# 1/rms of the first network handed over the partitions through DRAM, and its hidden products taken in later turns

## What is computed

```python
neighbor_sum = jnp.einsum('bnm,bmd->bnd', adjacency, x)
agg = epsilon * x + neighbor_sum
h = jnp.einsum('bnd,dh->bnh', agg, W1) + b1          # H = 512
h = jax.nn.silu(h * jax.lax.rsqrt(mean(h * h) + eps) * rms_weight)
out = jnp.einsum('bnh,hd->bnd', h, W2) + b2
x = _layernorm(x + out)
```

## Time and profile before

| | |
|---|---|
| runs | 1186.98 us median (1185.79 to 1189.19) |
| profiled execution | 1185.8 us, span of its instructions 1183.8 us |
| TensorE busy | 1129.8 us, 95% of the span |
| VectorE, ScalarE, GpSimd busy | 73%, 62%, 50% |
| mean granted TensorE clock | 0.984 of full speed |
| stage one | from 40.4 us (first `neighbours`) to 433.5 us |
| stage two | 433.5 us to 493 us |
| stage three | 494 us to the end |

### The profile page before, as it was taken

How to read it: one execution, slowest core, us unless ns; L and a number is a source line. 1 busy time by engine, 2 the same in 40 slices (tenths; PEclk the granted TensorE clock), 3 DMA queues, 4 the chain that set the end, 5 groups by cost and what they waited for, 6 DMA issues and landing times. The chain is left out here.

```text
span 1183.8 us, 24192 instructions
## 1 busy us (share of the span) xinstructions
PE 1129.8 (95%) x7851; PEld 1026.6 (87%) x7851; DVE 867.6 (73%) x2564; ACT 736.1 (62%) x1328; POOL 593.3 (50%) x528
## 2 busy tenths in 40 slices
PE   7899999999999879799999999999999999999984
PEld 7799999999999769678889899898989898989874
DVE  3378877777777713126878888888888888888984
ACT  3444455555555432156677778787878777787765
POOL 1044443434343226424565757575666666675754
PEclk9999999999999999979999999999999999999988
DMA  4123322232322134511011212121212121120001
GB/s 154 54 72 98 100 90 90 90 94 95 98 90 64 54 120 163 169 39 55 30 54 37 73 38 73 37 74 38 73 38 64 47 58 53 41 69 29 10 18 45
DMA packets 46962, 82.58 MB, mean 70 GB/s; under 512 B 5172, under 2 KB 15224, under 8 KB 46584
## 3 DMA queue, kind: packets, MB, share of 16 engines
q1 hardware_dynamic: 46840, 81.05, 21.7%
HBM read 55.34 MB, written 25.69 MB: 68 GB/s over the span
## 5 line engine op out<-in xcount | busy, mean ns | idle before, releaser
L162 POOL TENSOR_TENSOR rstd<-ve,minus_half 128x4 f32<-128x4 f32 x128 | 153.5, 1200 | 150.0 <-DVE ve L1012 144.3
L162 POOL TENSOR_TENSOR r_rms<-ms,minus_half 128x4 f32<-128x4 f32 x32 | 32.3, 1010 | 236.5 <-DVE ms L976 236.5
L454 PE MATMUL bank<-w,s 128*128 128x128 f32 x1024 | 135.1, 275 | 0.4 <-DVE y L990 0.4
L454 PEld LDWEIGHTS bank<-w,s 128*128 128x128 f32 x1024 | 126.9, 192 | 3.5 <-issue 0.5
L1322 POOL TENSOR_TENSOR edge_adj<-edge,atc 128x512 f32<-128x512 f32 x32 | 40.8, 1275 | 101.8 <-ACT edge L828 101.8
L755 ACT ACTIVATE s<-hn,cols 128x512 f32<-128x512 f32 x128 | 84.9, 712 | 10.9 <-DVE hn L983 10.3
L983 DVE SCALAR_TENSOR_TENSOR hn<-bank,cols,rv 128x512 f32<-128x512 f32 x128 | 86.8, 737 | 1.0 <-ACT rv L159 0.6
L149 PE MATMUL bank<-agg_hi,w_hi 128*128 128x512 f32 x192 | 86.9, 452 | 0.0
L1002 DVE BATCH_NORM_STATS2 stats<-y 128x6 f32<-128x128 f32 x384 | 82.7, 277 | 2.6 <-POOL y L1354 2.5
L155 PE MATMUL bank<-at,x_rows 128*128 128x128 f32 x512 | 71.3, 284 | 9.6 <-ACT x_rows L902 6.0
L155 PEld LDWEIGHTS bank<-at,x_rows 128*128 128x128 f32 x512 | 67.1, 199 | 14.1 <-ACT x_rows L902 7.3
(11 more groups left out here) (192 smaller groups left out, 3450.4 us busy)
## 6 DMA issues: line engine op xcount, KB each, us to landing
at<-in_at SPq DMA_DIRECT2D x32, 256.0 KB, 3.0
x_rows<-in_x SPq DMA_DIRECT2D x32, 256.0 KB, 2.9
ad<-in_ad SPq DMA_DIRECT2D x32, 256.0 KB, 2.7
x_scratch<-x SPq DMA_DIRECT2D x32, 256.0 KB, 3.2
x1c<-x_scratch SPq DMA_DIRECT2D x32, 256.0 KB, 2.6
atc<-in_at SPq DMA_DIRECT2D x32, 256.0 KB, 2.9
yh<-yh_scratch SPq DMA_DIRECT2D x32, 256.0 KB
out<-out_rows SPq DMA_DIRECT2D x32, 256.0 KB, 4.1
```

Of the source, the lines that this page charges most:

```text
L162: return nc.gpsimd.tensor_tensor(to[:], base[:], minus_half[:], ALU.pow)
L454: last = pe.matmul(bank[7][:, g, :], s[c][:, g, :], w2[:, c, :], start=(c == 0 and g == 0), stop=(c == H0 - 1), skip_group_check=True)
```

## The change

What it does:
- `spread_rms` goes, on TensorE and on ScalarE. Instead SyncE stores `r_rms` (128 x 4) to a DRAM scratch (`store_rms`) and loads its 2 KB back into every partition (`load_rv`, 128 x 2 KB) as `rv[p, n, g]`, in two buffers. `normalise` reads it as `p n g -> p g n`, so with a step of four elements (16 bytes).
- `agg_hi` and `agg_lo` get two buffers; `gram(t)` moves into the group's own turn, and the hidden products spread over turns k+1 and k+2, in a new order on every engine. `down`, `residual0`, `stats0`, `moments` and `apply0` come one turn later for a group; `x1_t`, `conv1` and `transform` stay at their distances. The PSUM banks are dealt anew.
- The row sums move from turn k+3 to k+12, and the load of the adjacency for them to turn k+11, with one buffer instead of two.
- `x` has five buffers instead of four. The staging tiles share memory with `hn`.
- Stage three: the order is as before; some `free` lists get further entries, of which none is reached when its first one exists, one wait on `ya` goes, and one empty turn at the end goes.

```diff
-        X_RING, AT_RING, AD_RING, X1_RING = 4, 2, 2, 2
+        X_RING, AT_RING, AD_RING, X1_RING, RV_RING = 5, 2, 1, 2, 2
...
+        rms_dram = nc.dram_tensor("rms_scratch", [GROUPS, P, G], F32, kind="Internal").ap()
...
-        rv = rows("rv")
+        agg_hi, agg_lo = ([rows(f"agg_{n}{i}", F32R) for i in range(2)] for n in ("hi", "lo"))
+        rv = [sb(f"rv{i}", [P, P, G]) for i in range(RV_RING)]
...
-        TURNS1 = GROUPS + 11
+        TURNS1 = GROUPS + 12
...
+            def store_rms(k):
+                until(sp, "r_rms", k)
+                landed(sp, rv_in, k - 2)
+                sp.dma_start(rms_dram[k], r_rms[:]).then_inc(rms_stored[k % 2], 16)
+
+            def load_rv(k):
+                landed(sp, rms_stored, k)
+                until(sp, "hn2", k - RV_RING)
+                sp.dma_start(rv[k % RV_RING][:], rms_dram[k].unsqueeze(0).to_broadcast([P, P, G])
+                             ).then_inc(rv_in[k % RV_RING], 16)
...
                     stage(load_x, t + 1)
+                stage(store_rms, t - 1)
+                stage(load_rv, t - 1)
+                stage(load_ad, t + 1 - 12)
                 stage(store_x1, t - 6)
-                stage(load_ad, t - 1)
...
             def gram(k):
-                free(pe, ("hn1", k - 1))
-                split_product(pe, flat(bank[0]), gram_hi[:], gram_lo[:], flat(agg_hi), flat(agg_lo),
+                free(pe, ("hcp", k - 8), ("ms", k - 1), ("prod", k - 1))
+                split_product(pe, flat(bank[5]), gram_hi[:], gram_lo[:], flat(agg_hi[k % 2]), flat(agg_lo[k % 2]),
...
-            def spread_rms(k):
-                until(pe, "r_rms", k)
-                free(pe, ("hcp", k - 7), ("rv", k - 1))
-                for g in range(G):
-                    last = pe.transpose(bank[4][:, g, :], r_rms[:, g:g + 1].to_broadcast([P, P]), ident[:])
-                last.then_inc(sem["spread"], 1)
...
             def hidden(k, c):
+                until(pe, "agg_hi", k)
+                until(pe, "agg_lo", k)
                 if c == 0:
-                    free(pe, ("hn0", k - 1))
+                    free(pe, ("xh0", k - 9), ("hn0", k - 1))
                 if c == 1:
-                    free(pe, ("prod", k))
+                    free(pe, ("xh1", k - 9), ("hn1", k - 1))
                 if c == 2:
-                    free(pe, ("ms", k))
+                    free(pe, ("hn2", k - 1))
                 if c == 3:
-                    free(pe, ("xh0", k - 9), ("hn3", k - 1))
+                    free(pe, ("hn3", k - 1))
...
             def conv1(k):
-                free(pe, ("rv", k + 6), ("hcp", k - 1))
+                free(pe, ("ms", k + 7), ("prod", k + 7), ("hcp", k - 1))
...
             def transform(k, half):
-                    free(pe, ("hn3", k + 8), ("xh0", k - 1))
+                    free(pe, ("hn0", k + 8), ("xh0", k - 1))
-                    free(pe, ("hn2", k + 8), ("xh1", k - 1))
+                    free(pe, ("hn1", k + 8), ("xh1", k - 1))
...
             for t in range(TURNS1):
                 stage(neighbours, t)
+                stage(down, t - 4, 3)
+                stage(hidden, t - 2, 3)
+                stage(square_sums, t - 1)
+                stage(hidden, t - 2, 2)
                 stage(conv1, t - 8)
+                stage(transform, t - 10, 1)
+                stage(down, t - 3, 0)
+                stage(hidden, t - 1, 1)
+                stage(transform, t - 10, 0)
+                stage(down, t - 3, 1)
+                stage(x1_t, t - 5)
+                stage(hidden, t - 1, 0)
                 stage(down, t - 3, 2)
-                stage(gram, t - 1)
-                stage(x1_t, t - 5)
-                stage(down, t - 3, 3)
-                stage(transform, t - 10, 0)
-                stage(transform, t - 10, 1)
-                stage(hidden, t - 1, 0)
-                stage(hidden, t - 1, 3)
-                stage(square_sums, t - 1)
-                stage(hidden, t - 1, 1)
-                stage(hidden, t - 1, 2)
-                stage(down, t - 2, 0)
-                stage(spread_rms, t - 1)
-                stage(down, t - 2, 1)
+                stage(gram, t)
...
-            def spread_rms(k):
-                until(act, "spread", k)
-                until(act, "hn2", k - 1)
-                copy(rv[:], bank[4][:]).then_inc(sem["rv"], 1)
...
             for t in range(TURNS1):
-                stage(x1_full, t - 6)
-                stage(silu, t - 2, 0)
-                stage(silu, t - 2, 1)
-                stage(spectrum_of, t - 10, 0)
-                stage(conv1, t - 9)
-                stage(spectrum_of, t - 10, 1)
-                stage(silu, t - 2, 2)
-                stage(silu, t - 2, 3)
+                stage(silu, t - 3, 2)
+                stage(silu, t - 3, 3)
                 stage(full, t)
                 stage(high, t)
-                stage(spread_rms, t - 1)
+                stage(x1_full, t - 6)
+                stage(spectrum_of, t - 10, 1)
+                stage(conv1, t - 9)
+                stage(spectrum_of, t - 10, 0)
+                stage(silu, t - 2, 1)
+                stage(silu, t - 2, 0)
...
             def normalise(k, c):
-                until(dve, "rv", k)
+                landed(dve, rv_in, k)
-                V.scalar_tensor_tensor(out=hn[c][:], in0=bank[(5, 0, 1, 3)[c]][:], scalar=column("b1", c), in1=rv[:],
+                V.scalar_tensor_tensor(out=hn[c][:], in0=bank[(3, 0, 2, 6)[c]][:], scalar=column("b1", c),
+                                       in1=rv[k % RV_RING][:].rearrange("p n g -> p g n"),
...
             for t in range(TURNS1):
+                stage(apply0, t - 5)
                 stage(product, t - 1)
-                stage(apply0, t - 4)
-                stage(residual0, t - 3)
+                stage(normalise, t - 3, 2)
+                stage(residual0, t - 4)
                 stage(mean_square, t - 1)
-                stage(stats0, t - 3)
-                stage(conv1_bias, t - 8)
-                stage(low, t)
-                stage(lambda k: moments(0, k, LN_EPS), t - 3)
-                stage(row_sums, t - 3)
-                stage(normalise, t - 1, 1)
-                stage(normalise, t - 1, 0)
-                stage(normalise, t - 1, 3)
-                stage(normalise, t - 1, 2)
+                stage(normalise, t - 2, 1)
+                stage(stats0, t - 4)
+                stage(low, t)
+                stage(normalise, t - 2, 0)
+                stage(moments, t - 4, 0, LN_EPS)
+                stage(normalise, t - 2, 3)
+                stage(row_sums, t - 12)
+                stage(conv1_bias, t - 8)
...
             def rms(k):
-                until(pool, "spread", k - 1)
+                landed(pool, rms_stored, k - 1)
...
                 stage(add_eps, t)
+                stage(norm, t - 5, 0)
                 stage(x_bias, t - 3)
-                stage(norm, t - 4, 0)
                 stage(rms, t - 1)
```

More of the change, by code:

```diff
@@ L45 @@
 FIRST_STEPS = """
-ae nb agg agg_hi agg_lo gram prod sums ms r_rms spread rv hid0 hid1 hid2 hid3 hn0 hn1 hn2 hn3
+ae nb agg agg_hi agg_lo gram prod sums ms r_rms hid0 hid1 hid2 hid3 hn0 hn1 hn2 hn3
 s0 s1 s2 s3 down0 down1 down2 down xb y0 moments0 r0 x1_rows x1t x1 c1 hcp hc dft0 dft1 xh0 xh1 row_sum
@@ L71, in graph_layers @@
         sem = {n: sem_of(n) for n in FIRST_STEPS + SECOND_STEPS + THIRD_STEPS}
-        X_RING, AT_RING, AD_RING, X1_RING = 4, 2, 2, 2
+        X_RING, AT_RING, AD_RING, X1_RING, RV_RING = 5, 2, 1, 2, 2
+        rms_stored, rv_in = ([sem_of(f"{n}{i}") for i in range(2)] for n in ("rms_stored", "rv_in"))
         x_in = [sem_of(f"x_in{i}") for i in range(2)]
@@ L186, in graph_layers @@
         ad = [rows(f"ad{i}") for i in range(AD_RING)]
-        agg, agg_hi, agg_lo = rows("agg"), rows("agg_hi", F32R), rows("agg_lo", F32R)
-        rv = rows("rv")
-        hn = [rows(f"hn{c}") for c in range(H0)]
+        agg = rows("agg")
+        agg_hi, agg_lo = ([rows(f"agg_{n}{i}", F32R) for i in range(2)] for n in ("hi", "lo"))
+        rv = [sb(f"rv{i}", [P, P, G]) for i in range(RV_RING)]
         x1_rows = rows("x1_rows")
@@ L192, in graph_layers @@
         hcp, hc = rows("hcp"), rows("hc")
-        y0 = rows("y0")
-        s = [rows(f"s{c}") for c in range(H0)]
-        stage_tile = [rows(f"stage{i}") for i in range(3)]
+        last_s, last_hn = rows("last_s"), rows("last_hn")
         xh = sb("xh", [P, HALVES, B])
         wh = sb("wh", [P, HALVES, P])
+        y0 = rows("y0")
+        s = [rows(f"s{c}") for c in range(H0 - 1)] + [last_s]
+        hn = [rows(f"hn{c}") for c in range(H0 - 1)] + [last_hn]
+        stage_tile = hn[0:3]
         w1f = flat(stage_tile[0])
@@ L464, in x1_t @@
                 for g in range(G):
-                    last = pe.transpose(bank[2][:, g, :], x1_rows[:, g, :], ident[:])
+                    last = pe.transpose(bank[1][:, g, :], x1_rows[:, g, :], ident[:])
                 last.then_inc(sem["x1t"], 1)
@@ L632, in gate_nmp @@
```

(21 more changed lines are left out.)

71 lines of the change are left out of this document (35 added, 36 removed).

## The result

| | before | after |
|---|---|---|
| median of 20 runs each, us | 1187.08 (1185.03 to 1192.57) | 1190.28 (1186.75 to 1195.81) |
| ratio | | 1.0026 [1.0014, 1.0039] |
| profiled execution, us | 1185.8 | 1195.8 |
| full turn of stage one, us | 11.57 | 11.54 (forecast 11.13 to 11.2) |
| stage two starts at, us | 433.56 | 430.51 (forecast 414.3) |

The account below looks back on a forecast made before the run. TensorE was taken to bound stage one's full turns, the chain between engines the last ones. Stage two 19.3 us earlier, plus 6.0 stop and 2.9 half clock, made -10.4 us from the median: 1176.5 us, range 1165 to 1194.

Parts of the forecast that it names:

- "I take no loss": `normalise` in stage one: reading `rv` with a 16-byte step costs nothing, judged from a PSUM copy at 1.04 ns per element.
- the rule against it: `normalise`'s read of `rv`: the Trainium skill says a different 16-byte SBUF line per access costs; no row showed it.
- a rival of 0.17: Stage one: strided reads lengthen each `normalise` by 0.53 us, VectorE becomes the bound, turn 11.8, total 1200; chance 0.17.
- Full turns: Stage one's 22 full turns: 0.44 us of TensorE work goes, 0.05 of waits comes, 11.13 us a turn; 8.6 us gained.
- First turns: Start of stage one: turn 3 at 58.5, turn 10 at 123.5 instead of 131.11, so 7.6 us ahead.
- Last turns: Turn 32 to stage two: 44.9 us instead of 48.0 by walking the new lists, so 3.1 us more gained.
- The late row sums: End of stage one: sums 3.45 us apart, the last ending 9.6 us after stage two's start, holding up GpSimd's weights.
- the stop: Stage two: TensorE waits for GpSimd's negated weight of slot 6, costing 6.0 us (5 to 7).
- the half clock: Stage two, after TensorE's long wait: matmuls at half speed cost 2.9 us; 3 to 8 if the clock falls, else nothing.
- The path of 1/rms: Full turns: store and broadcast load land by 11.7, `normalise` asks at 14.9; over 3 us of slack hide it.
- The late-1/rms rival: Stage one: 128 pieces of 16 bytes need 3 us more than the rows give; 1 us a turn gives 1208; chance 0.04.
- Stage three: Last stage: order the same, new entries behind ones taken first, empty turn without a step; costed at nothing.

Follow-up runs that it names:

- The probes: Changed kernel plus fourteen VectorE instructions of 400 elements before stage one, walking SBUF and PSUM with different steps; 1194.88 us in one run.
- the eleventh kernel: Changed kernel with `rv` read in memory order (values at wrong nodes) and row sums three turns after their group; 1169.65 us, 0.9833 of the kernel before.
- the first experiment: Changed kernel with `normalise` reading `rv` in memory order, values at wrong nodes, row sums still late; 1177.01 us, 0.9908 of the kernel before.
- the exchanged walk: Changed kernel with `normalise` going node by node: `rv` read in order, `hn` written with the step; 1186.55 us, with early row sums 1179.63.
- third experiment: Changed kernel with row sums three turns after their group instead of twelve, still one buffer; 1182.84 us, 0.9957 of the kernel before.

## Why the prediction was wrong, by its own steps

1. **The step that failed: "I take no loss"** for the read of `rv` in steps of 16 bytes. That term of the sum stood at nothing and measured 13.3 us. The prediction priced it by the only row with a step, a copy out of PSUM, named that as another memory, and put the rule against it aside with a rival of 0.17. The probes show that PSUM has no such price and SBUF has. A `normalise` becomes 0.39 us longer, 0.53 in the rival's reckoning. It costs 13.3 us (1190.3 to 1177.0; by the two ratios 14). Between the traces of after and of the eleventh kernel 5.3 us of it lie in the first turns, 7.1 in the 22 full ones and 1.0 in the last. The rival had the right mechanism, the right place (the half transform behind `hn0`, from 0.3 us each on) and the right side, but too large a bill: the turn became 11.54 and not 11.8, and the total rose by 3, not by 13. The table of rows had no evidence for "no loss": the honest weight between a row of another memory and a rule on this very one was nearer to even.
2. **Full turns.** The walk itself held. With the read in order a turn is 11.21 us, TensorE busy throughout: 0.08 above the list's 11.13, where 0.05 was taken.
3. **First turns.** Forecast for turn 10: 123.5; measured 130.69 with the strided read, and 125.38 in the eleventh kernel, which reads in order. There turns 3 to 9 take 7.96, 8.89, 9.27, 9.29, 9.27, 10.19 and 10.16, the forecast list; all of the missing 1.9 is in turns 0 to 2 (turn 3 at 60.35, forecast 58.5). The wait for the first 1/rms is not it: TensorE stands 1.0 + 0.3 us behind `normalise` in turn 2, where 1.6 was taken. But the matmuls keep the lengths of half clock (0.63 us, 0.39 later) until 53.17 and not 50.93, which makes about 1.1 us; the rest is open.
4. **Last turns.** Forecast from turn 32 to stage two: 44.9. In that kernel 125.38 + 22 x 11.21 = 372.0 to 417.07: 45.1. After itself has 46.0.
5. **The late row sums.** The mechanism was right link by link, and the sums come 3.4 us apart but for the one late load. With it the last one ended 11.6 us after stage two's start (9.6 forecast), the stop was 7.6 (5 to 7), and the half clock cost 2.9 (2.9, a figure under the prediction's own bounds of 3 to 8 and without a working). In the first experiment, without a late load, the three are 9.2, 5.2 and 2.4. In total the edit cost 7.4 us in this kernel, 7.4 with the read in order (1177.0 to 1169.65), 6.9 with the exchanged walk and 8.8 in the old kernel, all by medians (8.2, 8.9, 7.1 and 7.5 by the ratios), where the prediction had 8.9.
6. **The path of 1/rms** was hidden, as argued: VectorE waits 0.9 us for `rv` in the whole run. The late-1/rms rival is out for this store, and stands at once with 4-byte pieces.
7. **Stage three**: 693.4 us against 690.9 in the profiled executions, but 690.2 and 690.1 in the first and third experiment, with the same stage three: so nothing of the change.

The sum with the terms as measured: the forecast 1176.5 rises by 13.3 for the read and falls by 8.9 - 7.4 for the stop: 1188.3. The 1.9 us of turns 0 to 2, 0.7 of the full turns and 0.2 of the last ones make 1191.1. Measured 1190.28, which is as near as the medians of such runs allow. That the first experiment's 1177.01 lies so close to the forecast is in part luck: there stage two starts 4.2 us later than forecast, and what follows makes up for it.

## What to carry to other kernels

An access pattern is a price of its own: a step that leaves one element per 16 bytes of SBUF made fp32 instructions of VectorE and ScalarE and stationary loads of TensorE 40 to 90% longer here (0.37 to 0.52 us for a copy, 598 to 1118 ns for ScalarE's write), and where a transposition can be chosen it belongs on the engine with slack (here ScalarE), or in PSUM's walk, which cost VectorE nothing with steps of 400 and 512 bytes. Price it from a row of the same memory, and if there is none, don't take zero for it. A step that is moved late "because nothing needs it soon" must be followed to whoever waits for everything: here a row sum of no urgency stopped TensorE through GpSimd.

## What was unexpected of the hardware

- The three engines pay differently for the same 16-byte step: VectorE 0.39 us for 512 elements (735 to 1129 ns), ScalarE 0.50 to 0.52 (722 to 1221 reading, 598 to 1118 writing), a stationary load of 128 columns 0.135 (191 to 326 ns), of which 0.115 showed.
- In after a 2 KB row of DRAM spread over 128 partitions lands in 4.1 us, 256 KB with an address for each partition in 3.1 (2.7 in before).
- 2 KB stored in 512 pieces of 4 bytes lands in 9.8 us, in 128 pieces of 16 bytes in 1.5, and the load of `rv` behind it on the same queue goes from 4.1 to 5.2.
